# Expert weights in reading order, and one joined transfer for each contiguous stretch of the ring

## The chip, the cores and the metric

The kernel runs on one core of a Trainium2 chip. The metric is the time of one execution on the device in microseconds (us); it is measured in several runs and the median is given. A separate, profiled execution gives the trace.

## The reference, cut to what matters

One layer with 256 tokens of 512 numbers: cross-attention to a context of 4096 rows (16 heads), causal self-attention (16 heads), and a mixture of experts with 32 experts, of which each token chooses 4. The change concerns only how the weights of the experts come in. Each expert computes, for at most 10 rows gathered for it:

```python
G = jnp.einsum('ecd,edi->eci', Xp, W_gate)     # Xp (32, 10, 512), W_gate (32, 512, 256)
U = jnp.einsum('ecd,edi->eci', Xp, W_up)       # W_up (32, 512, 256)
Y = jnp.einsum('eci,eid->ecd', jax.nn.silu(G) * U, W_down)   # W_down (32, 256, 512)
Yf = Y.reshape(EC, d) * slots_w[:, None]
out = jnp.zeros((T, d), x.dtype).at[slots_token].add(Yf)
```

All of it is float32: 1.5 MB of weights an expert, 48 MB for 32 experts.

## The kernel before

The program is written out engine by engine. Five engines work through their own queues and wait for each other on semaphores. SyncE (SP) issues every load. A load adds 16 to its semaphore when all of it has landed.

**Layout of the weights.** The host lays out `w_exp` as (32 experts, 128 partitions, 3072 numbers): in each partition first the gate and up weights (`W_GU` = 2048 numbers, in four quarters of 512, one for each chunk `c` of 128 of the 512 input rows), then the down weights (2 × 512 numbers). So the gate/up part of one expert is 1 MB in 128 rows of 8 KB, a quarter of it is 256 KB in rows of 2 KB, and the down part is 512 KB in rows of 4 KB.

**Order of the experts.** The experts are read in groups of `GE` = 4, numbered by a reading index `k`; group `g` holds `k` = 4g to 4g+3. `expert(k)` (L116) says which expert is read as the `k`-th; it is a permutation, so neighbours in `k` are not neighbours in HBM.

**The ring.** SBUF has `RING` = 13 places for an expert's 3072 numbers a partition. Places 0 to 7 lie one after the other, 8 to 11 lie one after the other at another address, and 12 is by itself (L243). The expert with reading index `k` goes to place `k % 13`. Each place has a semaphore `ld_gu[k % 13]` for its gate/up part and `ld_down[k % 13]` for its down part (L319, L320).

**The loads** (SP, L400 to L449), one per expert and part:

- Places 0 to 7 after the cross-attention, 8 to 10 after its output product, 11 after the last transposes of the self-attention.
- Place 12 is shared with weights of the shared expert, so its load comes in pieces: the first half of gate/up once `sh_mm` is 1, the rest and the down part once `sh_mm` is 3.
- The other 19 experts (`k` = 13 to 31) refill freed places, in refill groups 0 to 4: `k` = 13-16, 17-20, 21-24, 25-28 and 29-31. Refill group `g` may be issued when TensorE has done group `g` (semaphore `gu_mm` for the gate/up part, `y_mm` for the down part). Group 0's gate/up parts are loaded a quarter at a time, as each chunk `c` of group 0 is done (`gu_part`). The order in the queue is: first half of `k` = 12, four quarters of group 0, gate/up of group 1, down of group 0, the rest of `k` = 12, down of group 1, gate/up and down of group 2, gate/up of groups 3 and 4, down of group 3, and last the down parts of group 4 in three parts (`END_PARTS`), three transfers each.

**Who reads them** (PE is TensorE). `gate_up(g, c)` (L1400) waits, for each of its four experts, for the gate/up semaphore of its place, in each of the four chunks `c`, and then multiplies at L1416. `down(g)` (L1432) waits for the down semaphores of its four experts and multiplies at L1444; for the last group it waits on `ld_end_down` part by part. Between the two, `hidden_back(g)` transposes the hidden values (L1429). The last stretch of TensorE's program is `gate_up(6)`, a part of the shared expert (L1369), `hidden_back(6)`, the adding of the rows (L1466, L1474), `gate_up(7)`, `down(6)`, `hidden_back(7)`, `down(7)`, and the combination (L1479). Group 6 is `k` = 24 to 27 and group 7 is `k` = 28 to 31.

Of the kernel before, what the change touches and what calls it, by code (L numbers as in the profile page):

```python
# [15 lines left out]
P = 128  # L16
# [3 lines left out]
DC = D // P  # L20
# [19 lines left out]
E = 32  # L40
# [4 lines left out]
GE = P // SLOT  # L45
NG = E // GE
W_GU = DC * 2 * FI
W_EXP = W_GU + FC * D
END_PARTS = [slice(W_GU, W_GU + D), slice(W_GU + D, W_GU + D + D // 2), slice(W_GU + D + D // 2, W_EXP)]
RING = 13  # L50
RING_LOW, RING_MID = 8, 11
# [1 line left out]
QK_BUFS, SM_BUFS, LAT_BUFS = 4, 5, 4  # L53
OUT_STEPS = H - LAT_BUFS
SH_FREES = 3
PIECED = GE
ENDING = RING + 4 * GE
XPW = E * CAP + SLOT - CAP
ROW_PARTS = [slice(0, 15), slice(15, E)]
# [56 lines left out]
def expert(k):  # L116

    trio, r = k // GE // 3, k // GE % 3
    each = min(3, NG - 3 * trio)
    return 12 * trio + each * (k % GE) + r  # L120


def gate_up_loaded(k):

    pieces = {RING - 1: 2, **{i: DC for i in range(RING, RING + PIECED)}}
    return 16 * sum(pieces.get(i, 1) for i in range(k % RING, k + 1, RING))


def wait(eng, sem, value):

    if isinstance(value, int) and value <= 0:
        return
    eng.wait_ge(sem, value)
# [12 lines left out]
def layer(nc, a, out):  # L146
    with ExitStack() as ctx:
        def sb(name, shape, dt=F32):
            return ctx.enter_context(nc.sbuf_tensor(name, shape, dt))
# [4 lines left out]
        def sem(name):  # L154
            return ctx.enter_context(nc.semaphore(name))
# [3 lines left out]
        arena = sb("arena", [P, 53200])  # L159

        def cut(cols, at=None):
            o = top[0] if at is None else at
            if at is None:
                top[0] += cols
            return arena[:, o:o + cols]
# [14 lines left out]
        q_at = top[0]  # L180
# [5 lines left out]
        r_at = top[0]  # L186
# [46 lines left out]
        high_at = r_at + (RING_MID - RING_LOW) * W_EXP  # L233
# [6 lines left out]
        rsum2 = arena[:, w_at + 1856:w_at + 1888].rearrange("p (s h) -> p s h", h=NH2)  # L240


        ring = [arena[:, o:o + W_EXP] for o in [W_EXP * e for e in range(RING_LOW)]  # L243
                + [r_at + W_EXP * e for e in range(RING_MID - RING_LOW)] + [high_at, q_at]]
        w_router = cut(DC * E).rearrange("p (c e) -> p c e", c=DC)
        bias_e = cut(E)
        sh_in = arena[:, q_at:q_at + 4096].rearrange("p (i n c k) -> p i n c k", i=DC, n=2, c=DC)
# [68 lines left out]
            sem(n) for n in ("q2_mm", "q2_done", "s2_mm", "s2_max", "s2_exp", "pT_mm", "pT_copied", "o2_mm", "o2_done",  # L316
                             "back_mm", "back_copied", "x2_mm"))
        ld_shared = [sem(f"ld_shared{i}") for i in range(2)]
        ld_gu = [sem(f"ld_gu{i}") for i in range(RING)]  # L319
        ld_down = [sem(f"ld_down{i}") for i in range(RING)]  # L320
        ld_end_down = [sem(f"ld_end_down{i}") for i in range(len(END_PARTS))]
        gu_part = sem("gu_part")
        cleared, logit_mm, sig_exp, sel_done, pos_mm, oh_done, ow_done, xp_mm, xp_copied = (
# [11 lines left out]
        def _(sp):  # L335
# [61 lines left out]
            sp.wait_ge(ctx_done, H)  # L397
            sp.dma_start(wo2, a["w_o2"]).then_inc(ld_wo2, 16)

            def load_expert(k, part, done):  # L400
                sp.dma_start(ring[k % RING][:, part], a["w_exp"][expert(k)][:, part]).then_inc(done[k % RING], 16)
            gate_up, down = slice(0, W_GU), slice(W_GU, W_EXP)

            def load_whole(k):
                load_expert(k, gate_up, ld_gu)
                load_expert(k, down, ld_down)
            for k in range(RING_LOW):
                load_whole(k)
            sp.wait_ge(o1_mm, OUT_STEPS + TT)
            for k in range(RING_LOW, RING_MID):  # L410
                load_whole(k)
            sp.wait_ge(q2_mm, NH2)
            sp.dma_start(sh_in, a["w_shared_in"].rearrange("p (i n c k) -> p i n c k", i=DC, n=2, c=DC)).then_inc(ld_shared[0], 16)
            sp.wait_ge(pT_mm, NH2)
            load_whole(RING_MID)
            sp.wait_ge(x2_mm, TT + 1)
            sp.dma_start(sd, a["w_shared_out"].rearrange("p (c n) -> p c n", c=DC)).then_inc(ld_shared[1], 16)
            def new(g):
                return range(RING + GE * g, min(RING + GE * (g + 1), E))

            def load_group(g, part, freed, done):
                sp.wait_ge(freed, g + 1)
                for k in new(g):
                    load_expert(k, part, done)
            quarters = [slice(2 * FI * c, 2 * FI * (c + 1)) for c in range(DC)]
            sp.wait_ge(sh_mm, 1)
            load_expert(RING - 1, slice(0, W_GU // 2), ld_gu)
            for c in range(DC - 1):
                sp.wait_ge(gu_part, c + 1)
                for k in new(0):  # L430
                    load_expert(k, quarters[c], ld_gu)
            load_group(0, quarters[DC - 1], gu_mm, ld_gu)
            load_group(1, gate_up, gu_mm, ld_gu)
            load_group(0, down, y_mm, ld_down)
            sp.wait_ge(sh_mm, SH_FREES)
            load_expert(RING - 1, slice(W_GU // 2, W_GU), ld_gu)
            load_expert(RING - 1, down, ld_down)
            load_group(1, down, y_mm, ld_down)
            last = (E - RING) // GE
            for g in range(2, last - 1):  # L440
                load_group(g, gate_up, gu_mm, ld_gu)
                load_group(g, down, y_mm, ld_down)
# [2 lines left out]
            load_group(last - 1, down, y_mm, ld_down)  # L445
            sp.wait_ge(y_mm, last + 1)
            for i, part in enumerate(END_PARTS):
                for k in new(last):
                    sp.dma_start(ring[k % RING][:, part], a["w_exp"][expert(k)][:, part]).then_inc(ld_end_down[i], 16)  # L449
            for n in range(2):  # L450
                half = slice(D // 2 * n, D // 2 * (n + 1))
                sp.wait_ge((x3_done, x3_second)[n], 1)
# [542 lines left out]
        def _(pe):  # L995
# [212 lines left out]
            for h in range(H + 2):  # L1208
# [3 lines left out]
                if 1 <= h <= H:  # L1212
                    g = h - 1
# [3 lines left out]
                if h >= 2:  # L1217
                    last = projected(h - 2, 0)
# [4 lines left out]
            for g in range(OUT_STEPS, H):  # L1223
                last = projected(g, TT - 1)
# [6 lines left out]
            for st in range(TT):  # L1231
# [109 lines left out]
            for st in range(TT):  # L1341
# [5 lines left out]
                for c in range(DC):  # L1347
                    last = mm(psA[0][:, E * st:E * st + E], xnT[:, c, P * st:P * st + P], w_router[:, c, :], start=c == 0, stop=c == DC - 1)
# [51 lines left out]
            def gate_up(g, c):  # L1400

                if g == 0:
                    pe.wait_ge(xp_copied, c + 1)
                    if c == 0:
                        pe.wait_ge(sh_done, 1)
                elif g == 3 and c == 0:
                    pe.wait_ge(xp_copied, 2 * DC)
                if c == 0:
                    wait(pe, hid_done, g - 1)
                for j in range(GE):  # L1410
                    k = GE * g + j
                    pe.wait_ge(ld_gu[k % RING], gate_up_loaded(k))
                for j in range(GE):
                    k = GE * g + j
                    e = expert(k)
                    last = mm(psF[g % 2][SLOT * j:SLOT * j + SLOT, :], xpT[:, c, CAP * e:CAP * e + SLOT], ring[k % RING][:, 2 * FI * c:2 * FI * (c + 1)],  # L1416
                              start=c == 0, stop=c == DC - 1)
                if c == DC - 1:
                    last.then_inc(gu_mm, 1)
                elif g < PIECED // GE:  # L1420
                    last.then_inc(gu_part, 1)

            def hidden_back(g):
# [8 lines left out]
            def down(g):  # L1432
                trio = g // 3
                pe.wait_ge(hT_copied, g + 1)
                wait(pe, y_copied, min(trio, TRIOS - 1))
                for j in range(GE):
                    k = GE * g + j
                    if k < ENDING:
                        pe.wait_ge(ld_down[k % RING], 16 * (k // RING + 1))
                def product(c, bank, out):  # L1440
                    for j in range(GE):
                        k = GE * g + j
                        o = W_GU + D * c
                        last = mm(bank[SLOT * j:SLOT * j + SLOT, out], hT[g % 3][:, c, SLOT * j:SLOT * j + SLOT], ring[k % RING][:, o + out.start:o + out.stop],  # L1444
                                  start=g % 3 == 0 and c == 0, stop=(g % 3 == 2 or g == NG - 1) and c == FC - 1, skip_group_check=True)
                    return last
                for c in range(FC):
                    if g == NG - 1 and c == 0:
                        pe.wait_ge(ld_end_down[0], 16 * (E - ENDING))
                    if trio < TRIOS - 1:  # L1450
                        last = product(c, psA[trio % 2], slice(0, D))
                    else:
                        for n in range(2):
                            if g == NG - 1 and c == FC - 1:
                                pe.wait_ge(ld_end_down[1 + n], 16 * (E - ENDING))
                            last = product(c, psA[n], halves[n])
                            if g == NG - 1 and c == FC - 1:
                                last.then_inc(y_mm, 1)
                if g < NG - 1:
                    last.then_inc(y_mm, 1)  # L1460
# [91 lines left out]
def lay_out(i):  # L1552
    g = {k: np.asarray(v) for k, v in i.items()}
    const, rope = constants()
    arrays = {"x": g["x"], "const": const, "rope": rope}
# [17 lines left out]
    pe = qb[:, :, NOPE:]  # L1573
# [9 lines left out]
    arrays["w_shared_out"] = shared[2].reshape(P, -1)  # L1583
    up = [g[f"L0_ffn_W_{n}"].reshape(E, DC, P, FI) for n in ("gate", "up")]
    down = g["L0_ffn_W_down"].reshape(E, FC, P, D).transpose(0, 2, 1, 3).reshape(E, P, -1)
    arrays["w_exp"] = np.concatenate([np.concatenate(up, 3).transpose(0, 2, 1, 3).reshape(E, P, -1), down], 2)
    return {k: np.ascontiguousarray(v) for k, v in arrays.items()}


# [11 lines left out]
```

## Time and profile before

| | us |
|---|---|
| median of 3 runs | 651.63 (649.9 to 651.67) |
| the profiled execution | 650.6 |
| its span (first to last instruction) | 648.7 |
| TensorE busy | 625.1 (96% of the span) |
| experts' multiplications, L1416 | 29.5 |

The profiled execution's own time is 1.9 us more than its span. A trace gives for every instruction its start and length, what ended the idle time before it, and for a load the time from its issue to its landing. A window's DMA share is the mean busy share of the 16 DMA engines, and GB/s is what they moved.

### The profile page before, as it was taken

Reading aid. Unit: us, or ns where it says so; the run is one execution under the profiler, and the core shown is the slowest. Engines: PE = TensorE matmul, PEld = TensorE weight load, DVE = VectorE, ACT = ScalarE, POOL = GpSimd, SP = SyncE. Lnnn points to the kernel's source line nnn. Section 1 sums busy time; section 2 is a strip of 40 time slices with the busy share of each in tenths; the row PEclk is TensorE's granted clock in tenths of the full one; section 3 lists DMA queues with packets and bytes.
Section 4 is the critical chain, followed back from the end, with each engine's and each line's share of the span. In section 5 each row is a group of like instructions: output and inputs, shape, how many; then the busy total and the mean of one; then the engine's idle time right before and its main releaser. Section 6 shows DMA issues by size and latency. Waiting matters only on the chain.

```text
span 648.7 us, 15224 instructions
## 1 busy us (share of the span) xinstructions
PE 625.1 (96%) x6035; PEld 466.0 (72%) x6035; DVE 378.8 (58%) x571; ACT 362.0 (56%) x494; POOL 177.7 (27%) x146
## 2 busy tenths in 40 slices
PE   7999999999999999999999999999999999999976
PEld 5986676777777778777777777899556897564443
DVE  5888587866767767767677676655214565501000
ACT  3543665777676677667667676788122874311000
POOL 0270334353453443443444434300000331000000
PEclk7999999999999999999999999999999999999999
DMA  8944884223423422422522521600999107499996
GB/s 338 419 171 94 219 317 98 58 56 74 82 51 65 90 49 59 99 49 51 107 49 43 116 50 36 125 2 3 379 417 371 80 2 250 151 398 411 420 417 224
DMA packets 28648, 105.14 MB, mean 162 GB/s; under 512 B 4288, under 2 KB 8896, under 8 KB 23488
## 3 DMA queue, kind: packets, MB, share of 16 engines
q1 hardware_dynamic: 28608, 104.57, 50.5%
q8 instruction: 30, 0.49, 0.3%
q14 instruction: 10, 0.08, 0.0%
HBM read 77.29 MB, written 0.52 MB: 120 GB/s over the span
## 4 chain that ended last, share of the span: by engine, by line
PE 82%; DVE 6%; issue 4%; ACT 3%; DMA 2%; SPq 2%; POOL 0%; DVEq 0%
PE psO L1128 9%; PE psO L1139 9%; PE psO L1129 8%; PE psS L1115 8%; PE psS L1116 8%; PE psM L1087 5%; PE psO L1207 4%; PE psS L1416 3%; PE psO L1071 3%; PE psS L1050 3%; PE psO L1042 2%; DVE arena L783 2%; SPq L449 2%; PE psO L1073 2%; PE psO L1072 2%
## 5 line engine op out<-in xcount | busy, mean ns | idle before, releaser
L783 DVE TENSOR_REDUCE arena<-psM 128x2 f32<-128x1024 f32 x121 | 147.7, 1221 | 67.4 <-PE psM L1087 67.1
L589 ACT ACTIVATE arena<-psS 128x1024 bf16<-128x1024 f32 x128 | 131.3, 1026 | 87.6 <-PE psS L1116 85.4
L482 POOL TENSOR_TENSOR arena<-arena 128x1024 bf16<-128x1024 f32 x56 | 120.8, 2156 | 190.4 <-ACT arena L591 166.9
L1128 PE MATMUL psO<-arena 128*128 128x129 bf16 x1024 | 132.8, 220 | 0.3 <-DVE arena L801 0.3
L1129 PE MATMUL psO<-arena 128*128 128x128 bf16 x1024 | 132.4, 220 | 0.0
L591 ACT ACTIVATE arena<-psS 128x1024 f32<-128x1024 f32 x129 | 131.0, 1017 | 0.0
L1115 PE MATMUL psS<-arena 128*128 128x256 bf16 x512 | 120.5, 273 | 0.9 <-DVE arena L794 0.9
L1116 PE MATMUL psS<-arena 65*128 65x256 bf16 x512 | 120.8, 273 | 0.0
L1128 PEld LDWEIGHTS psO<-arena 128*128 128x128 bf16 x1024 | 99.1, 98 | 18.8 <-issue 11.2
L1129 PEld LDWEIGHTS psO<-arena 128*128 128x128 bf16 x1024 | 99.4, 97 | 6.7
L822 DVE TENSOR_TENSOR arena<-arena 128x1024 bf16<-128x1024 f32 (+1 forms) x73 | 88.0, 1207 | 15.4 <-ACT arena L591 15.3
L1139 PE MATMUL psO<-arena 128*128 128x129 bf16 x1024 | 79.0, 220 | 0.2
L1139 PEld LDWEIGHTS psO<-arena 128*128 128x128 bf16 x1024 | 65.7, 97 | 2.8 <-DVE arena L822 1.1
L1115 PEld LDWEIGHTS psS<-arena 128*128 128x128 bf16 x512 | 50.2, 98 | 7.4 <-DVE arena L716 1.0
L1116 PEld LDWEIGHTS psS<-arena 65*128 65x128 bf16 x512 | 50.0, 98 | 5.4
L581 ACT CAST arena<-psO 128x512 bf16<-128x512 f32 x64 | 37.8, 591 | 24.5 <-PE psO L1073 24.3
L777 DVE TENSOR_TENSOR arena<-psO,arena 128x512 bf16<-128x512 f32 x64 | 43.8, 684 | 12.1 <-ACT arena L581 11.3
L1087 PE MATMUL psM<-arena 64*128 64x512 bf16 x242 | 47.2, 386 | 2.5 <-DVE arena L783 1.6
L1416 PE MATMUL psS<-arena 128*32 128x512 f32 x256 | 29.5, 595 | 4.2 <-DMA arena<-w_exp 4.2
L980 DVE TENSOR_TENSOR arena<-psS,arena 128x256 f32<-128x256 f32 x8 | 3.4, 424 | 47.1 <-ACT arena L670 47.1
L1207 PE MATMUL psO<-arena 128*128 128x512 f32 x64 | 30.2, 594 | 0.0
L1087 PEld LDWEIGHTS psM<-arena 64*128 64x128 bf16 x242 | 11.6, 93 | 22.5 <-issue 10.3
(209 smaller groups left out, 740.5 us busy)
## 6 DMA issues: line engine op xcount, KB each, us to landing
arena<-w_exp SPq DMA_DIRECT2D x27, 1024.0 KB, 19.6
arena<-arena SPq DMA_DIRECT2D x96, 256.0 KB, 3.7
arena<-w_exp SPq DMA_DIRECT2D x31, 512.0 KB, 16.8
arena<-w_pair SPq DMA_DIRECT2D x7, 1088.0 KB, 18.3
arena<-w_exp SPq DMA_DIRECT2D x19, 256.0 KB, 6.0
arena<-w_o SPq DMA_DIRECT2D x1, 4096.0 KB, 18.2
arena<-ctx SPq DMA_DIRECT2D x4, 512.0 KB, 13.1
arena<-rope SPq DMA_DIRECT2D x4, 512.0 KB, 13.9
```

Of the source, the lines that this page charges most:

```text
L482: nc.gpsimd.tensor_tensor(p_lo[:, s % 2, :], p_f[:, s % 2, :], p_hi[:, s % 2, :], ALU.subtract).then_inc(s_plo[0], 1)
L589: nc.scalar.activation(p_hi[:, s % 2, :], psS[s % 2][:, :], ACT.Exp).then_inc(s_phi, 1)
L591: nc.scalar.activation(p_f[:, s % 2, part], psS[s % 2][:, part], ACT.Exp).then_inc(s_pf, 1)
L783: nc.vector.reduce_max(maxes[:, :, st, c], maxima_bank(q, m)[:, :].rearrange("p (j n) -> p j n", j=2), AX.X).then_inc(s_mfree, 1)
L822: nc.vector.tensor_tensor(p_lo[:, s % 2, part], p_f[:, s % 2, part], p_hi[:, s % 2, part], ALU.subtract).then_inc(s_plo[s % 2], 1)
L1087: last = mm(bank[:, 512 * j:512 * j + 512], queries_of[r, P * st:P * st + P], k_hi[r, 512 * c:512 * c + 512], start=True, stop=True)
L1115: mm(o, k1[:, j, l], q1[:, j, :], start=True, stop=False)
L1116: last = mm(o, k2[0:R + 1, j, l], q2[0:R + 1, j, :], start=False, stop=True)
L1128: mm(psC[:, st, :], ph, vx[:, GROUP * g + i, 0:CW], start=g == 0 and i == 0 and st == 0, stop=False, skip_group_check=True)
L1129: last = mm(psC[:, st, 0:K], ph, vx[:, GROUP * g + i, CW:VW], start=False, stop=False, skip_group_check=True)
L1139: last = mm(psC[:, st, :], p_lo[:, s % 2, T * i + P * st:T * i + P * st + P], vx[:, GROUP * g + i, 0:CW], start=False, stop=g == HALF - 1 ...
L1207: return mm(psO[st][:, :], latT[:, g % LAT_BUFS, P * st:P * st + P], wo1[:, g, :], start=g == 0, stop=g == H - 1)
```

## The change

The host stores the experts in reading order, so that `k` is the index in HBM. The ring's stretches that are contiguous in SBUF and filled together become runs, `(first, end)`: (0,4), (4,8), (8,11), (11,12), (12,13) at the start, and then (13,17), (17,21), (21,25), (25,26) and (26,29), (29,32), one refill group each except the fourth, which goes over the ring's end. One transfer loads the same part of all experts of a run. A run has one semaphore for gate/up and one for down, and its readers wait for the run's transfer at the first expert of each group and at the first expert of each run. `SP`'s waits for freed places and the order of the transfers in the queue stay.

```diff
-def gate_up_loaded(k):
+def refills(g):
+
+    ks = range(RING + GE * g, min(RING + GE * (g + 1), E))
+    turn = [k for k in ks if k % RING == 0 and k > ks[0]]
+    return [(ks[0], turn[0]), (turn[0], ks[-1] + 1)] if turn else [(ks[0], ks[-1] + 1)]
+
+REFILLS = [refills(g) for g in range((E - RING + GE - 1) // GE)]
+RUNS = [(0, GE), (GE, RING_LOW), (RING_LOW, RING_MID), (RING_MID, RING - 1), (RING - 1, RING)] + [run for group in REFILLS for run in group]
+
+def run_of(k):
+
+    return next(first for first, end in RUNS if first <= k < end)
+
+def gate_up_loaded(first):
 
-    pieces = {RING - 1: 2, **{i: DC for i in range(RING, RING + PIECED)}}
-    return 16 * sum(pieces.get(i, 1) for i in range(k % RING, k + 1, RING))
+    pieces = {RING - 1: 2, RING: DC}
+    return 16 * sum(pieces.get(f, 1) for f, _ in RUNS if f <= first and f % RING == first % RING)
+
+def down_loaded(first):
+
+    return 16 * sum(1 for f, _ in RUNS if f <= first and f % RING == first % RING)
...
-            def load_expert(k, part, done):
-                sp.dma_start(ring[k % RING][:, part], a["w_exp"][expert(k)][:, part]).then_inc(done[k % RING], 16)
+            def load_run(run, part, done):
+                first, end = run
+                o = ring_at[first % RING]
+                places = arena[:, o:o + W_EXP * (end - first)].rearrange("p (k w) -> p k w", w=W_EXP)
+                sp.dma_start(places[:, :, part], a["w_exp"][first:end, :, part].rearrange("k p w -> p k w")).then_inc(done, 16)
...
-            for k in range(RING_LOW):
-                load_whole(k)
+            for run in RUNS[0:2]:
+                load_whole(run)
...
                 sp.wait_ge(freed, g + 1)
-                for k in new(g):
-                    load_expert(k, part, done)
+                for run in REFILLS[g]:
+                    load_run(run, part, done[run[0] % RING])
...
             for i, part in enumerate(END_PARTS):
-                for k in new(last):
-                    sp.dma_start(ring[k % RING][:, part], a["w_exp"][expert(k)][:, part]).then_inc(ld_end_down[i], 16)
+                load_run(REFILLS[last][0], part, ld_end_down[i])
...
-                    pe.wait_ge(ld_gu[k % RING], gate_up_loaded(k))
+                    if j == 0 or run_of(k) == k:
+                        pe.wait_ge(ld_gu[run_of(k) % RING], gate_up_loaded(run_of(k)))
...
-                    if k < ENDING:
-                        pe.wait_ge(ld_down[k % RING], 16 * (k // RING + 1))
+                    if k < ENDING and (j == 0 or run_of(k) == k):
+                        pe.wait_ge(ld_down[run_of(k) % RING], down_loaded(run_of(k)))
...
-                        pe.wait_ge(ld_end_down[0], 16 * (E - ENDING))
+                        pe.wait_ge(ld_end_down[0], 16)
...
-    arrays["w_exp"] = np.concatenate([np.concatenate(up, 3).transpose(0, 2, 1, 3).reshape(E, P, -1), down], 2)
+    arrays["w_exp"] = np.concatenate([np.concatenate(up, 3).transpose(0, 2, 1, 3).reshape(E, P, -1), down], 2)[[expert(k) for k in range(E)]]
```

## Rows read from the trace of the kernel before

**Rows 1.** The page: its span, part 1's TensorE row, part 2's DMA slices.
```profile
span 648.7 us, 15224 instructions
...
PE 625.1 (96%) x6035; PEld 466.0 (72%) x6035; DVE 378.8 (58%) x571; ACT 362.0 (56%) x494; POOL 177.7 (27%) x146
...
DMA  8944884223423422422522521600999107499996
```

**Rows 2.** Waits of TensorE, 556 to 649 us: total us, times, longest.
```profile
PE psS L1416 <- DMA arena<-w_exp: 4.2, 2, 3.5
...
PE psM L1444 <- DMA arena<-w_exp: 1.5, 3, 1.0
```

**Rows 3.** Chain that ended last, 618 to 649 us: start, us, what.
```profile
633.63 9.21 DMA arena<-w_exp
642.85 0.04 issue
642.89 0.64 PE psM L1444 x8
```

**Rows 4.** Windows: engines' busy us, clock, DMA share, GB/s.
```profile
510.00:520.00 10.00, 10.00 (x71) 9.12 (x70) 6.57 (x26) 7.67 (x17) 2.88 (x4) 1.00 0.00 0
...
563.00:565.00 2.00, 2.00 (x18) 0.87 (x20) 0.00 (x0) 0.39 (x2) 0.00 (x0) 1.00 0.65 199
565.00:571.00 6.00, 6.00 (x58) 1.76 (x54) 0.42 (x1) 1.07 (x4) 0.00 (x0) 1.00 0.99 324
571.00:575.00 4.00, 4.00 (x30) 2.58 (x23) 0.42 (x1) 0.33 (x2) 0.00 (x0) 1.00 1.05 397
...
588.00:598.00 10.00, 8.71 (x67) 4.83 (x69) 1.54 (x3) 1.51 (x4) 0.00 (x0) 1.00 1.03 410
600.00:609.00 9.00, 9.00 (x67) 4.46 (x66) 0.33 (x1) 0.61 (x2) 0.00 (x0) 1.00 1.01 418
...
641.00:642.00 1.00, 1.00 (x20) 0.54 (x24) 0.00 (x0) 0.00 (x0) 0.00 (x0) 1.00 0.12 41
```

**Rows 5.** DMA of 557 to 643 us: packets and bytes, the instruction queue.
```profile
DMA packets 8501, 31.54 MB, mean 367 GB/s; under 512 B 944, under 2 KB 1712, under 8 KB 6576
...
q8 instruction: 5, 0.08, 0.4%
```

**Rows 6.** Timeline of SP, five single issues: start, us, then the issue.
```profile
1.19 0.42 SPq L346 DMA_DIRECT2D arena<-x  x1
...
600.69 0.43 SPq L401 DMA_DIRECT2D arena<-w_exp  x1
...
601.17 6.30 SPq L401 DMA_DIRECT2D arena<-w_exp  x1
...
610.00 1.05 SPq L401 DMA_DIRECT2D arena<-w_exp  x1
...
615.74 0.44 SPq L401 DMA_DIRECT2D arena<-w_exp  x1
```

**Rows 7.** The last four's issue to landing, in their order: KB, us.
```profile
arena<-w_exp SPq DMA_DIRECT2D x1, 1024.0 KB, 23.1
...
arena<-w_exp SPq DMA_DIRECT2D x1, 1024.0 KB, 25.1
...
arena<-w_exp SPq DMA_DIRECT2D x1, 1024.0 KB, 23.7
...
arena<-w_exp SPq DMA_DIRECT2D x1, 512.0 KB, 23.1
```

**Rows 8.** Timeline of TensorE, 618 to 649 us: start, us, line, count, [idle before].
```profile
618.46 1.93 PE L1444 MATMUL psM<-arena 128*32 128x512 f32 x16 [0.32 <-ACT arena L678]
...
623.89 3.64 PE L1416 MATMUL psS<-arena 128*32 128x512 f32 x32 [3.51 <-DMA arena<-w_exp]
...
633.84 3.64 PE L1416 MATMUL psS<-arena 128*32 128x512 f32 x32 [0.71 <-DMA arena<-w_exp]
...
637.67 1.93 PE L1444 MATMUL psM<-arena 128*32 128x256 f32 x32 [0.20 <-DMA arena<-w_exp]
639.53 0.44 PE L1429 MATMUL psS<-arena 128*128 128x128 f32 x2
...
640.96 1.57 PE L1444 MATMUL psM<-arena 128*32 128x256 f32 x24 [0.99 <-DMA arena<-w_exp]
...
643.46 2.00 PE L1479 MATMUL psO<-arena 128*128 128x256 f32 x8
```

More of the change, by code:

```diff
@@ L55 @@
 SH_FREES = 3
-PIECED = GE
 ENDING = RING + 4 * GE
@@ L240, in layer @@
         rsum2 = arena[:, w_at + 1856:w_at + 1888].rearrange("p (s h) -> p s h", h=NH2)
-        ring = [arena[:, o:o + W_EXP] for o in [W_EXP * e for e in range(RING_LOW)]
-                + [r_at + W_EXP * e for e in range(RING_MID - RING_LOW)] + [high_at, q_at]]
+        ring_at = [W_EXP * e for e in range(RING_LOW)] + [r_at + W_EXP * e for e in range(RING_MID - RING_LOW)] + [high_at, q_at]
+        ring = [arena[:, o:o + W_EXP] for o in ring_at]
         w_router = cut(DC * E).rearrange("p (c e) -> p c e", c=DC)
@@ L318, in layer @@
         ld_shared = [sem(f"ld_shared{i}") for i in range(2)]
-        ld_gu = [sem(f"ld_gu{i}") for i in range(RING)]
-        ld_down = [sem(f"ld_down{i}") for i in range(RING)]
+        starts = sorted({first % RING for first, _ in RUNS})
+        ld_gu = {i: sem(f"ld_gu{i}") for i in starts}
+        ld_down = {i: sem(f"ld_down{i}") for i in starts}
         ld_end_down = [sem(f"ld_end_down{i}") for i in range(len(END_PARTS))]
@@ L398, in _, with load_whole @@
             sp.dma_start(wo2, a["w_o2"]).then_inc(ld_wo2, 16)
-            def load_expert(k, part, done):
-                sp.dma_start(ring[k % RING][:, part], a["w_exp"][expert(k)][:, part]).then_inc(done[k % RING], 16)
-            gate_up, down = slice(0, W_GU), slice(W_GU, W_EXP)
-            def load_whole(k):
-                load_expert(k, gate_up, ld_gu)
-                load_expert(k, down, ld_down)
-            for k in range(RING_LOW):
-                load_whole(k)
+            def load_run(run, part, done):
[3 more added lines that the diff above has]
+                sp.dma_start(places[:, :, part], a["w_exp"][first:end, :, part].rearrange("k p w -> p k w")).then_inc(done, 16)
+            gate_up, down = slice(0, W_GU), slice(W_GU, W_EXP)
+            def load_whole(run):
+                load_run(run, gate_up, ld_gu[run[0]])
+                load_run(run, down, ld_down[run[0]])
+            for run in RUNS[0:2]:
+                load_whole(run)
             sp.wait_ge(o1_mm, OUT_STEPS + TT)
-            for k in range(RING_LOW, RING_MID):
-                load_whole(k)
+            load_whole(RUNS[2])
             sp.wait_ge(q2_mm, NH2)
@@ L414, in _ @@
             sp.wait_ge(pT_mm, NH2)
-            load_whole(RING_MID)
+            load_whole(RUNS[3])
             sp.wait_ge(x2_mm, TT + 1)
             sp.dma_start(sd, a["w_shared_out"].rearrange("p (c n) -> p c n", c=DC)).then_inc(ld_shared[1], 16)
-            def new(g):
-                return range(RING + GE * g, min(RING + GE * (g + 1), E))
             def load_group(g, part, freed, done):
                 sp.wait_ge(freed, g + 1)
-                for k in new(g):
-                    load_expert(k, part, done)
+                for run in REFILLS[g]:
+                    load_run(run, part, done[run[0] % RING])
+            held = (RING - 1, RING)
             quarters = [slice(2 * FI * c, 2 * FI * (c + 1)) for c in range(DC)]
             sp.wait_ge(sh_mm, 1)
-            load_expert(RING - 1, slice(0, W_GU // 2), ld_gu)
+            load_run(held, slice(0, W_GU // 2), ld_gu[RING - 1])
             for c in range(DC - 1):
                 sp.wait_ge(gu_part, c + 1)
-                for k in new(0):
-                    load_expert(k, quarters[c], ld_gu)
+                load_run(REFILLS[0][0], quarters[c], ld_gu[0])
             load_group(0, quarters[DC - 1], gu_mm, ld_gu)
@@ L435, in _ @@
             sp.wait_ge(sh_mm, SH_FREES)
-            load_expert(RING - 1, slice(W_GU // 2, W_GU), ld_gu)
-            load_expert(RING - 1, down, ld_down)
+            load_run(held, slice(W_GU // 2, W_GU), ld_gu[RING - 1])
+            load_run(held, down, ld_down[RING - 1])
             load_group(1, down, y_mm, ld_down)
-            last = (E - RING) // GE
+            last = len(REFILLS) - 1
             for g in range(2, last - 1):
@@ L1419, in gate_up @@
                     last.then_inc(gu_mm, 1)
-                elif g < PIECED // GE:
+                elif g == 0:
                     last.then_inc(gu_part, 1)
@@ L1454, in down @@
                             if g == NG - 1 and c == FC - 1:
-                                pe.wait_ge(ld_end_down[1 + n], 16 * (E - ENDING))
+                                pe.wait_ge(ld_end_down[1 + n], 16)
                             last = product(c, psA[n], halves[n])
```

## The prediction

> **What bounds the kernel now.** I read the page first: TensorE is busy in 96% of the span of 648.7 us, but the DMA digits are 9 in the slices before the last [rows 1]. So there may be a stage in which TensorE is nearly full and the loads set the end. The waits of the last 93 us name it: TensorE stands 4.2 us at L1416 and 1.5 us at L1444 for `w_exp` and hardly anywhere else [rows 2]. The chain that ended last goes from the last weights transfer, issued at 633.63 and landed at 642.85, straight into the last eight multiplications [rows 3]. The windows say how full the stream of weights is: from 565 us on, the DMA share is 1.0, at 324, then 397, 410 and 418 GB/s [rows 4]. Between 557 and 643 us, 31.5 MB go through, 20 experts' weights [rows 5]. Even at 418 GB/s these take 75 us, so the end is the start of this stream, plus bytes over rate, plus some 6 us of work behind the last landing. TensorE is late only in its last two groups: group 6 starts at 623.89 after 3.51 us of waiting, group 7 at 633.84 after 0.71 us [rows 8]. The first 11 experts are no matter: from 510 to 520 us the DMA share is 0.00, everything issued until then has landed [rows 4], and no wait on them is among [rows 2].
>
> **The change part by part.** The rows of 8, 4 and 2 KB stay what they are, in each expert's own 12 KB rows; what is joined is four transfers of 128 rows into one of 512. The sum is made on the profiled execution (650.6 us).
>
> *Fewer transfers.* 557 to 643 us has 944 small packets, 16 a transfer, so 59 transfers [rows 5]. After: first half of `k` = 12 (1), four quarters (4), groups 1 (2), 0's down (1), rest of `k` = 12 (2), group 2 (2), group 3 in two runs (4), group 4's gate/up (1), the last three parts (3): 20. So 39 go. What does a transfer cost beside its bytes? A 1 MB one at 418 GB/s (600 to 609 us) takes 2.51 us, 512 KB at 410 (588 to 598) takes 1.28, 256 KB at 397 (571 to 575) takes 0.66 [rows 4]. Halving leaves 2 × 1.28 − 2.51 = 0.05 us, and 2 × 0.66 − 1.28 = 0.04 us. This fixed part belongs to the transfer or to its 128 rows, for each engine has 8 rows and one small packet of each. If all is the transfer's, 39 × 0.05 = 1.9 us are gained; if all is the rows', nothing. I take it as spread evenly over the nine packets: 39 × 0.05 / 9 = 0.2 us gained.
>
> The Trainium skill weighs in here ("DMA: Bandwidth & Descriptors", the section on the anatomy of one DMA, and its rules for kernel authors): some 2.0 us fixed for each DMA, and many small transfers are to be coalesced. Taken as a cost of each transfer in the stream it would give 78 us for the 39, more than the whole stream; these rows show transfers queued behind each other, with 0.05 us between them, so here that cost is latency, which the queue hides.
>
> *The start of the stream.* The four quarters of group 0 are now four issues and not sixteen. They move 324 GB/s from 565 to 571 us where later 2 KB rows move 397 [rows 4]: 6 × (397 − 324) = 0.44 MB, or 1.1 us late; from 563 to 565 us, 2 × (397 − 199) = 0.40 MB, 1.0 us late. If SP's issues were the cause, up to 2.1 us would come back, and everything behind would land that much earlier. But the share in 565 to 571 is 0.99 [rows 4]: the engines were not idle, their packets took longer, which a quicker issue doesn't mend. I take 0.3 us. On the other side, one transfer of 512 rows could be slower to begin: if its issue of 0.43 us grew with the rows, the first would come 1.3 us later. The load of `x`, 256 rows in one issue, took 0.42 us, no longer than one of 128 rows (0.43) [rows 6], so I put this at nothing and keep 1.3 us as the loss end.
>
> *The coarser waits.* Now a group also waits for experts of the next group that share its run: group 4 for `k` = 20, group 5 for 24, group 6 for 28. For groups 4 and 5 all has long landed, as TensorE does not wait there [rows 2]. In group 6 it counts. Before, `k` = 27 landed at 600.69 + 23.1 = 623.8 and L1416 began at 623.89. `k` = 28 landed at 601.17 + 25.1 = 626.3 [rows 6, 7], 2.5 us later, so group 6 begins at 626.4. What follows without a wait takes 633.84 − 0.71 − 623.89 = 9.24 us [rows 8], so group 7 begins at 635.6, not 633.84 (its own weights landed at 610.00 + 23.7 = 633.7 [rows 6, 7]): 1.8 us late. Then 3.6 us at L1416: `down(6)` can start at 639.2. It now needs `k` = 28's down part too, landed at 615.74 + 23.1 = 638.8 [rows 6, 7]: no wait. It takes 1.86 us (637.67 to 639.53), the transposes 0.38, their way over ScalarE back to L1444 0.32 [rows 8]: `down(7)` starts at 641.8 and not 640.96, and its first 24 multiplications, 1.57 us before, end at 643.4, its last eight at some 643.7 against 643.53. The copy of the first half of its result takes 0.4 us on VectorE, so the combination starts at about 643.8 against 643.46 [rows 8]. Lost: 0.3 us. So 2.5 us of new wait are nearly swallowed by the waits for the last parts (0.99 and 0.36 us) and the 0.91 us that group 7 and `down(6)` stood. Bounds: 0 and, if nothing swallowed it, 2.5. If the stream gets earlier by d, both limits move by d, and so does the end.
>
> *Waits and instructions on TensorE.* 157 waits become 74. They lie beside multiplications in progress (L1416 has no idle but for DMA [rows 2]), so they cost nothing before or after. 83 instructions fewer move the moments at which instructions are fetched: five packets of 16 KB in these 86 us [rows 5], each 16384 B / (418 GB/s / 16) = 0.6 us of one engine. The last landing is one engine's: at 641 to 642 us the share is 0.12, two engines of 16 [rows 4]. So whether such a packet meets the latest engine moves the end by 0.6 us either way; I take nothing.
>
> *HBM layout.* An engine now goes from a row to the same row of the next expert, 1.5 MB on, before the next partition 12 KB on. No row of this trace has such a stride, so its nearest bounds are the rates of this stream itself: 418 GB/s, unchanged, and 397, the lowest that a full share shows late in it [rows 4]. All engines step to the next expert together, so the distances between engines stay; I take no change. Joined are 18 of 20 experts, 28.3 MB: 68.2 us at 415, 71.3 at 397, so 3.1 us is the loss end.
>
> The skill's page "DMA: Bandwidth & Descriptors", section "Latency and other measured facts", speaks against the change: copies with a row pitch of 512 KiB ran at 207 GB/s and of 2 MiB at 164, with a padded pitch at 214. Taken over to this stride, an estimate from that page is 3 to 30% more time for the joined loads, 2 to 20 us. No row here can show it; it was measured for the pitch between partitions, which here stays 12 KB.
>
> Sum: 650.6 − 0.2 − 0.3 + 0.3 = 650.4. The profiled execution was 1.03 us below the median of the runs, so as a median 651.63 − 0.2 = 651.4 us.
>
> **The rivals.**
>
> *The stream starts earlier.* SP's sixteen short issues did hold the early quarters back: −2.1 − 0.2 + 0.3 = −2.0, 649.6 us. For it: 199 and 324 GB/s just where the issues are dense; against it: the share of 0.99.
>
> *The fixed part is the transfer's.* −1.9 − 0.3 + 0.3 = −1.9, 649.7 us. For it: it is the same 0.04 to 0.05 us at three sizes; against it: the rows a transfer are the same at all three.
>
> *Slower: rows 1.5 MB apart come at a lower rate.* Price up to 3.1 us, with the 0.3 us of waiting and the 0.2 gained 3.2: 654.8 us. It decides from a loss of 2.7% of the rate on, which is 1.9 us; it would show in all windows from 577 us on.
>
> *Not joined.* The three-dimensional transfer is split again into one per expert. The gain of 0.2 and of the start is lost, the wait stays: +0.3, 651.9 us. Against it: `x` is loaded in two rows a partition in one issue [rows 6].
>
> **How the numbers follow.** Forecast 0.59, earlier start 0.12, fixed part 0.10, slower rate 0.13, not joined 0.06. A measurement of this kernel tells a change from none at about 0.3%, 2.0 us (below 649.7, above 653.6). The first two rivals lie on that edge and pass it if they come together with each other or with a lucky instruction fetch: 0.20 for faster, with a little from the forecast's own spread. Slower is the fourth case, 0.13. The forecast's own range is 650.0 to 652.8 (the terms' 0.3 us, the fetch's 0.6 us, the coarser wait, the median's own spread). The range for 8 in 10 goes down to the two faster rivals and a bit below, 648.9, and up into the rate loss, 653.8.
>
> **What would show it.** Right: 20 issues of `w_exp` from 557 us on; 416 to 422 GB/s where 8 KB rows run; L1416 of group 6 starts about 2.5 us after its old distance to the stream, with an idle of some 6 us; L1444's waits for DMA near zero; the last landing within 1 us of 642.9. The 0.3 us of the start is wrong if 565 to 571 us shows some 397 GB/s. The prediction fails if the rate from 577 us on differs by over 2%, if TensorE waits in group 4 or 5, or if a joined transfer leaves engines idle while SP stands in its issue.

## The result, and the profile after

| | before | after |
|---|---|---|
| median, 22 runs each, beside each other | 649.51 us (648.17 to 651.67) | 651.63 us (649.3 to 653.34) |
| ratio of the runs | | 1.0021, 95% interval 1.0011 to 1.0031 |
| profiled execution; its span | 650.6; 648.7 | 650.83; 649.0 |

The change makes the kernel slower: by the ratio of the runs 0.2% or 1.4 us (0.7 to 2.0 by its interval); the medians lie 2.1 us apart, the means 1.6 (649.65 and 651.20 us). The ratio lies within the 0.3% that the forecast took for "no change", but its interval excludes 1, and the forecast had it 0.2 us faster. The median that the forecast started from (3 runs) was itself 2 us above that of 22 runs; what counts is the difference.

The two spans differ by 0.3 us only, because the two executions began differently. In the first 18 us the granted clock was lower for longer in the profile of before: the mean from 7 to 18 us is 0.53 before, 0.69 after (windows; the granted clock, as a share of 2.4 GHz, is the third number from the end). Before:

```profile
7.00:18.00 11.00, 8.86 (x34) 7.83 (x34) 6.70 (x16) 4.05 (x7) 2.02 (x1) 0.53 1.02 417
```

After:

```profile
7.00:18.00 11.00, 9.29 (x48) 7.96 (x48) 7.42 (x17) 5.94 (x10) 1.84 (x1) 0.69 1.03 412
```

This hides 1.1 us. So all profiles are compared below from one common point, the issue of the first quarter of refill group 0: 562.51 us before, 561.43 after. From there to the end of the span it is 86.2 us before and 87.6 after, 1.4 us more. Two more profiles of each kernel, below, give 86.6 and 86.0 before, 87.0 and 87.1 after, so that the means of three lie 1.0 us apart.

SP's timeline (start, us) of the kernel after: the first quarter, the fourth, the gate/up run (26, 29), and the last part.

```profile
561.43 0.39 SPq L425 DMA_DIRECT2D arena<-w_exp  x1
...
565.70 0.38 SPq L425 DMA_DIRECT2D arena<-w_exp  x1
...
598.40 0.44 SPq L425 DMA_DIRECT2D arena<-w_exp  x1
...
627.02 4.31 SPq L425 DMA_DIRECT2D arena<-w_exp  x1
```

And the way to landing of the last three of these (KB, us):

```profile
arena<-w_exp SPq DMA_DIRECT2D x1, 1024.0 KB, 9.7
...
arena<-w_exp SPq DMA_DIRECT2D x1, 3072.0 KB, 26.1
...
arena<-w_exp SPq DMA_DIRECT2D x1, 384.0 KB, 14.1
```

The last part lands at 627.02 + 14.1 = 641.1, 79.7 us after the first issue; before it was 642.85 − 562.51 = 80.3 [rows 3]. The loads got earlier, by 0.7 us. What got longer is the way from the last landing to the end: 5.9 us before, 7.9 after. TensorE's timeline says why (start, us, idle before in brackets; L1436 was L1416, L1464 was L1444, L1388 was L1369, L1499 was L1479; the rows answer to [rows 8]):

```profile
624.61 5.45 PE L1436 MATMUL psS<-arena 128*32 128x512 f32 x32 [5.30 <-DMA arena<-w_exp]
629.99 2.00 PE L1388 MATMUL psO<-arena 128*128 128x256 f32 x8
...
635.59 3.64 PE L1436 MATMUL psS<-arena 128*32 128x512 f32 x32
639.05 1.91 PE L1464 MATMUL psM<-arena 128*32 128x256 f32 x32
...
641.64 1.93 PE L1464 MATMUL psM<-arena 128*32 128x256 f32 x32 [0.32 <-ACT arena L697]
643.76 2.00 PE L1499 MATMUL psO<-arena 128*128 128x256 f32 x8 [0.18 <-DVE arena L996]
```

Group 6 waits 5.30 us and not 3.51, as its wait is now for `k` = 28 too (598.40 + 26.1 = 624.5). Then its 32 multiplications take 5.45 us, not 3.64. The windows show the granted clock (third number from the end), in the idle time and in the work behind it:

```profile
620.00:621.00 1.00, 0.00 (x0) 0.00 (x0) 0.07 (x1) 0.00 (x0) 0.00 (x0) 1.00 0.98 410
621.00:622.00 1.00, 0.00 (x0) 0.00 (x0) 0.00 (x0) 0.00 (x0) 0.00 (x0) 0.74 1.01 418
622.00:623.00 1.00, 0.00 (x0) 0.00 (x0) 0.00 (x0) 0.00 (x0) 0.00 (x0) 0.50 1.04 434
...
625.00:626.00 1.00, 1.00 (x8) 0.23 (x4) 0.00 (x0) 0.00 (x0) 0.00 (x0) 0.50 0.98 410
...
629.00:630.00 1.00, 1.00 (x13) 0.15 (x5) 0.00 (x0) 0.00 (x0) 0.00 (x0) 1.00 0.97 397
```

TensorE goes idle at 619.3; from 621.5 on its clock is granted at half, 1.2 and not 2.4 GHz; it resumes at 624.6 and has the full clock back only at 628.3. In the kernel before, the clock was at 1.00 from 616 to 630 us, its 3.5 us of idle time included. The multiplications of group 7, of `down(6)` and `down(7)` then have no wait on `w_exp` left: the waits of 0.71, 0.20, 0.99 and 0.36 us that stood there before are used up.

### The profile page after: what moved, and what is told of

Its sections match the earlier page's. It is cut to its first block, busy times and chain, and to the rows that moved or that the text cites. A ratio compares the mean times of both kernels' runs of the same rounds, so it can differ in the third digit from the quotient of the medians.

```text
span 649.0 us, 15126 instructions
## 1 busy us (share of the span) xinstructions
PE 626.6 (97%) x6035; PEld 466.0 (72%) x6035; DVE 379.5 (58%) x571; ACT 361.9 (56%) x494; POOL 178.6 (28%) x146
## 4 chain that ended last, share of the span: by engine, by line
PE 82%; DVE 6%; DMA 5%; issue 4%; ACT 3%; SPq 0%; POOL 0%; DVEq 0%
PE psO L1147 9%; PE psO L1158 9%; PE psO L1148 8%; PE psS L1134 8%; PE psS L1135 8%; PE psM L1106 5%; DMA arena<-w_exp 4%; PE psO L1226 4%; PE psS L1436 4%; PE psO L1090 3%; PE psS L1069 3%; DVE arena L802 2%; PE psO L1061 2%; PE psO L1092 2%; PE psO L1091 2%
## 5 line engine op out<-in xcount | busy, mean ns | idle before, releaser
L1436 PE MATMUL psS<-arena 128*32 128x512 f32 x256 | 31.3, 626 | 5.3 <-DMA arena<-w_exp 5.3
```

## The experiments

Theory A: the coarser wait of group 6 costs the time, for the most part through the TensorE clock, which falls in the longer idle time. Rival B: the joined transfers themselves cost it. Rival C: group 6's later start costs it by itself, whatever the clock. Each experiment was timed beside the kernel before, and its ratio is to that. "From the first quarter" means: span, less the issue of the first quarter.

### The coarser wait alone

```diff
                     pe.wait_ge(ld_gu[k % RING], gate_up_loaded(k))
+                if g == 6:
+                    pe.wait_ge(ld_gu[28 % RING], gate_up_loaded(28))
```

> The kernel before, all transfers as before, with one wait more: group 6's gate/up multiplications (L1416) also wait for the gate/up part of k = 28. Theory A (the loss is the coarser wait, and most of it the TensorE clock, which falls in the longer idle time and makes group 6's multiplications take 5.4 us and not 3.6): idle before group 6 some 5.9 us, granted clock 0.50 in part of it, L1416 x32 at 5.4 us, time 1.5 to 2.1 us over the kernel before. Rival B (the joined transfers themselves cost the time, the wait is swallowed as forecast): 0 to 0.3 us over the kernel before.

Measured: ratio 1.0029 (1.0015 to 1.0043), medians 651.52 against 649.81. From the first quarter 87.4 us, within 0.2 us of the changed kernel. Its timeline (L1418 was L1416) and its clock from 616 to 630 us:

```profile
625.99 5.21 PE L1418 MATMUL psS<-arena 128*32 128x512 f32 x32 [5.42 <-DMA arena<-w_exp]
```
```profile
616.00:630.00 14.00, 8.26 (x54) 3.31 (x54) 1.11 (x2) 0.61 (x2) 0.00 (x0) 0.88 1.01 420
```

One wait more, with all 59 transfers as before, makes the whole loss. Rival B falls. The clock fell later here than in the first profile of the changed kernel: at 625.8 us, 0.2 before TensorE resumed.

### The run cut at `k` = 28

```diff
+REFILLS[3] = [(25, 26), (26, 28), (28, 29)]
```

> The changed kernel with the run (26, 29) cut into (26, 28) and (28, 29), so that group 6 waits for its own experts alone. Theory A: idle before group 6 some 3.0 us (3.5 before, less what the stream gained at its start), granted clock 1.00 in 616 to 630, L1436 x32 at 3.6 us; time 1.5 to 2.1 us below the changed kernel, 0.3 to 0.7 below the kernel before. Rival B: time stays at the changed kernel's, 1.4 us over the kernel before.

Measured: ratio 0.9991 (0.9979 to 1.0003), median 648.76. From the first quarter 85.2 us, 2.4 less than the changed kernel. The wait is shorter, as expected, but the clock fell here too, against the expectation (L1437 was L1416, L1465 was L1444):

```profile
621.67 5.13 PE L1437 MATMUL psS<-arena 128*32 128x512 f32 x32 [2.46 <-DMA arena<-w_exp]
...
632.34 3.64 PE L1437 MATMUL psS<-arena 128*32 128x512 f32 x32
...
638.79 1.53 PE L1465 MATMUL psM<-arena 128*32 128x256 f32 x24 [0.72 <-DMA arena<-w_exp]
640.67 0.64 PE L1465 MATMUL psM<-arena 128*32 128x256 f32 x8 [0.36 <-DMA arena<-w_exp]
```

It cost nothing that the profile shows: the last parts are still waited for behind it (0.72, 0.36 us), and the end comes 5.84 us after the last landing, as before (5.87). So the fall is dear only where the slack in front of the last landing has been spent.

### The wait filled

```diff
             for g in range(2, NG):
+                if g == 6:
+                    warm(22, psF[1])
```

`warm(n, psF[1])` issues n bf16 multiplications that need no load and whose results are overwritten later.

> The changed kernel with 22 bf16 multiplications of 128 x 128 by 128 x 512 (results overwritten later) ahead of group 6's wait, some 4.7 us of work in the 5.3 us of idle time; no wait is shortened. Theory A with the clock as its cause: granted clock 1.00 throughout, L1436 x32 at 3.6 us, time 1.8 us below the changed kernel, some 0.4 below the kernel before. Rival C (the later start of group 6 costs the 1.4 us by itself, whatever the clock): time within 0.4 us of the changed kernel.

Measured: ratio 1.0000 (0.9987 to 1.0012), median 650.03. The filling is L1020:

```profile
620.61 4.92 PE L1020 MATMUL psS<-arena 128*128 128x512 bf16 x22
626.18 3.64 PE L1436 MATMUL psS<-arena 128*32 128x512 f32 x32 [0.66 <-DMA arena<-w_exp]
```
```profile
616.00:630.00 14.00, 13.03 (x85) 5.58 (x82) 1.12 (x2) 0.73 (x3) 0.00 (x0) 1.00 1.01 421
```

Group 6 starts as late as in the changed kernel (63.4 us after the first quarter, there 63.2), the clock is full, and the kernel is as fast as the one before. Rival C falls: the late start is nearly harmless, the clock is what hurts. The end comes 6.15 us after the last landing, against 5.87 before and 7.89 in the changed kernel.

### Only the four quarters joined

```diff
-                for k in new(0):
-                    load_expert(k, quarters[c], ld_gu)
+                load_quarter(c)        # one transfer for k = 13 to 16, weights in reading order
```

> The kernel before with the experts stored in reading order and only the four quarters of refill group 0 joined (16 transfers are 4); all other transfers and all waits as before. If the start of the stream gains because SP no longer spends sixteen issues on it: landing of the last quarter 14.0 us after the first issue instead of 14.5, last landing 0.5 us earlier counted from that issue, time 0.3 to 0.6 us below the kernel before. If the gain needs all transfers joined: landings as before, time within 0.2 us of the kernel before.

Measured: ratio 1.0000 (0.9987 to 1.0014), median 649.51. The last quarter landed 14.7 us after the first issue, not earlier than before (14.5), so four issues in place of sixteen did not speed up the quarters here. Yet the last landing was at 79.2 us, as early as in kernels with all transfers joined. One profile doesn't settle a term this small; what all of them say together is below.

### Cut and filled; the kernel before, filled

The cut kernel with `warm(10, psF[1])` ahead of group 6, and the kernel before with `warm(14, psF[1])` there.

> The changed kernel with the run (26, 29) cut at 28, and 10 bf16 multiplications (2.2 us, results overwritten later) ahead of group 6's wait. If the clock's fall in that idle time is the only loss left, which the cut alone still showed in its profile (3.4 us at 0.50 after 2.5 us of idle time): clock 1.00, L1436 x32 of group 6 at 3.6 us, time 0 to 1.0 us below the cut alone (648.8), 1.0 to 1.8 us below the kernel before. If the fall there is harmless because the last transfers swallow it: time as with the cut alone, within 0.3 us.

> The kernel before with 14 bf16 multiplications (3.1 us) in its own 3.5 us of idle time ahead of group 6. Its runs lie between 648.3 and 652.0 us with different mean clocks. If part of that spread is a clock that falls in this idle time: median 0.3 to 0.7 us below the kernel before and fewer runs at a mean clock of 0.989 or less. If its spread comes from the start of the program alone: same median within 0.2 us.

Measured: 0.9992 (0.9975 to 1.0009), median 649.81, and 1.0002 (0.9988 to 1.0017), median 650.44, beside 650.22 of the kernel before. Both profiles have L1416's 32 at 3.64 us and a clock of 1.00. Neither gains anything that intervals of about 1 us to each side would show; the gain of 1.0 us or more that was expected of the first did not come. Where the last parts are waited for, a clock held up is worth little.

### Filled in part, at the beginning of the wait

`warm(8, psF[1])` in the changed kernel.

> The changed kernel with 8 bf16 multiplications (1.8 us) at the beginning of group 6's idle time, which leaves 3.5 us of it idle, as long as before. If the loss grows with the idle time that TensorE has before group 6: clock falls in some runs only, median between the changed kernel (651.6) and the one with the wait filled (650.0), some 650.5 us. If any work in the wait is enough: 650.0. If filling must be complete: 651.6.

Measured: ratio 1.0023 (1.0006 to 1.0039), median 651.43: as the changed kernel.

```profile
620.37 1.90 PE L1020 MATMUL psS<-arena 128*128 128x512 bf16 x8
625.16 5.34 PE L1436 MATMUL psS<-arena 128*32 128x512 f32 x32 [2.89 <-DMA arena<-w_exp]
```

2.89 us of idle time behind the filling went with a fall, less than the 3.51 us that the first profile of the kernel before went through at full clock. The clock fell at 625.8 us, 0.6 after TensorE had resumed. It is not a matter of the idle time's length alone.

### The changed kernel once more, and the kernel before twice more

> The changed kernel, unaltered, profiled once more. Theory A: end of group 6's multiplications late by the clock (L1436 x32 at 4.5 to 5.5 us), or, in a run of mean clock 0.992 or more, at 3.6 us with a span some 1.8 us shorter than the first profile's. Rival B: L1436 at 3.6 us and the span no shorter.

> The kernel before, unaltered, profiled once more. If its 3.5 us of idle time never bring the clock down: L1416 of group 6 at 3.6 us, clock 1.00 from 18 us to its end. If they do in part of the runs, this one may show 5.2 us, with a span over 1 us longer counted from the first quarter's issue.

> As the run above, a third profile of the kernel before; the same two readings.

Measured, from the first quarter to the end: 87.0 us for the changed kernel. Its clock fell at 624.4 us, 0.2 after TensorE had resumed, and the 32 multiplications took as much longer:

```profile
624.22 5.34 PE L1436 MATMUL psS<-arena 128*32 128x512 f32 x32 [4.88 <-DMA arena<-w_exp]
```
```profile
624.00:625.00 1.00, 0.78 (x8) 0.29 (x12) 0.00 (x0) 0.00 (x0) 0.00 (x0) 0.69 1.04 434
625.00:626.00 1.00, 1.00 (x12) 0.42 (x8) 0.00 (x0) 0.00 (x0) 0.00 (x0) 0.50 0.94 393
```

For the kernel before 86.6 and 86.0. The second profile of it shows the clock falling in its own 3.4 us of idle time:

```profile
624.22 6.33 PE L1416 MATMUL psS<-arena 128*32 128x512 f32 x32 [3.42 <-DMA arena<-w_exp]
...
636.08 3.64 PE L1416 MATMUL psS<-arena 128*32 128x512 f32 x32
```
```profile
616.00:630.00 14.00, 10.27 (x62) 3.71 (x58) 1.12 (x2) 0.61 (x2) 0.00 (x0) 0.76 1.01 421
```

The third does not (L1416 at 3.64 us). So the kernel before meets the same fall in part of its executions. It makes L1416 2.7 us longer, and the end 0.3 and 0.6 us later than in the two profiles without it, since 2.3 us of waits for weights stood behind it.

### The filling put behind the wait for group 6's own weights

```diff
+                if g == 6 and c == 0:
+                    warm(10, psF[1])
+                    pe.wait_ge(ld_gu[28 % RING], gate_up_loaded(28))
```

> The kernel before with the coarser wait of group 6 for k = 28, and 10 bf16 multiplications (2.2 us) between the arrival of group 6's own weights and that wait: 3.5 us idle as in the kernel before, then busy until k = 28 has landed. If idle time beyond that of the kernel before is what brings the clock down: L1416 x32 of group 6 at 3.6 us in most runs, time within 0.3 us of the kernel before. If 3.5 us of idle time and a later start are enough: L1416 at 5.2 us, time 1 to 1.5 us over the kernel before.

Measured: ratio 1.0012 (0.9994 to 1.0030), median 651.49: inconclusive by the time. The profile shows the fall at 622.6 us, in the idle time, and the filling itself (L1001) at the low clock:

```profile
623.45 4.42 PE L1001 MATMUL psS<-arena 128*128 128x512 bf16 x10 [2.93 <-DMA arena<-w_exp]
627.81 4.40 PE L1419 MATMUL psS<-arena 128*32 128x512 f32 x32
```

Ten multiplications take 4.42 us, where ten took 2.33 at full clock in the cut kernel, and `k` = 28 had landed at 625.8: filling that comes after the fall makes group 6 later still, 88.5 us from the first quarter, the longest of all.

### What joining is worth, with the wait filled in both

The kernel before with the coarser wait and `warm(22, psF[1])`, one transfer per expert. It differs from the changed kernel with its wait filled in two things at once, the joined transfers and the order of the experts in HBM.

> The kernel before, its transfers one per expert, with the coarser wait of group 6 for k = 28 and 22 bf16 multiplications (4.9 us) ahead of it: the same wait and the same filling as the changed kernel with its wait filled (1.0000 of the kernel before), so that the two differ in the joined transfers and the order in HBM alone. If joining is worth nothing: clock 1.00, ratio to the kernel before 0.999 to 1.001. If joining gives what the forecast had in it (0.5 us): 0.3 to 0.7 us over the kernel before, that is about 1.0008. If it gives the 2 us of the faster rivals: over 1.0025.

Measured: 1.0015 (0.9996 to 1.0034), median 650.39 beside 650.15; which by itself tells little. Four kernels were then timed on one chip, beside each other: the changed one, the changed one filled, this one, and the cut one.

> The changed kernel, timed beside the three below. If the clock's fall before group 6 costs it 1.1 to 1.6 us as the profiles say: 0.7 to 1.6 us over f2, with more runs of a mean clock of 0.989 or less.

> The changed kernel with 22 bf16 multiplications in group 6's wait, timed beside f3, which has the same wait and filling with one transfer per expert. If joining and the order in HBM are worth nothing: within 0.3 us of f3. If joining is worth the forecast's 0.5 us or more: that much below f3.

> One transfer per expert, coarser wait of group 6, 22 bf16 multiplications in it. Worth of joining nothing: as f2. Worth 0.5 us: 0.5 us over f2. Worth 2 us, as the two faster rivals had it: 2 us over f2.

> The changed kernel with its run (26, 29) cut at 28. If the coarser wait is the whole loss: 1.0 to 2.0 us below f1 and, with the wait of the kernel before, 0 to 0.8 us below the kernel before. If the loss were in the joined transfers: as f1.

| on one chip | median | ratio to before (649.82) |
|---|---|---|
| changed (7 runs) | 652.31 | 1.0046 (1.0029 to 1.0062) |
| changed, wait filled (12) | 649.88 | 1.0002 (0.9988 to 1.0016) |
| one transfer per expert, same wait, filled (12) | 650.75 | 1.0014 (1.0000 to 1.0028) |
| changed, cut at 28 (12) | 650.01 | 1.0007 (0.9989 to 1.0026) |

The profile of the changed kernel taken here is its third: 87.1 us from the first quarter, L1436's 32 at 5.34 us behind 4.98 us of idle time. Filling the wait takes 2.4 us off the changed kernel, more than the 0.7 to 1.6 that were expected, the cut 2.3; the intervals of the changed kernel and of the filled one lie apart. Joining and the order in HBM together are worth 0.9 us by the medians, with intervals that overlap. The mean clock of the runs is a rough count of the falls, since it also holds the low clock at the program's start, whose length varies: at 0.989 or less were 40 of 117 runs of the kernel before, 20 of 29 of the changed one, 7 of 12 with the coarser wait alone, but 1 of 47 in the four timings with 22 fillers in the same wait; of the cut kernel, 9 of 23. It misses some: the second and the third profile of the changed kernel show a fall at a mean clock of 0.992 and 0.995. Among the 22 runs of the changed kernel, the 6 at 0.992 have a mean of 649.7 us, the 11 at 0.989 one of 651.5, the 5 at 0.987 one of 652.4; part of these steps is the start's.

## Why the prediction was wrong

*The step that failed* is in "the coarser waits": "What follows without a wait takes 633.84 − 0.71 − 623.89 = 9.24 us". These 9.24 us, from the start of group 6 to that of group 7, begin with group 6's 32 multiplications at L1416, 3.64 us in a row behind 3.51 us of idle time at a granted clock of 1.00. The forecast put them behind 6 us of idle time as if the clock came along. In all five profiles with the coarser wait and nothing or 1.9 us of filling ahead of it (the changed kernel three times, the wait alone, the wait filled in part) the 32 took 5.2 to 5.5 us, and the stretch 10.7 to 11.0. In the four with the wait filled they took 3.64, and the stretch 9.2. The "3.6 us at L1416" of group 7 held in all of them. The missing term is 1.6 us at the end: it comes 7.7 to 7.9 us after the last landing in the five, and 5.9 to 6.2 in the four.

The wait itself was right in kind and forecast too long. Group 6 was to begin 2.5 us later; counted from the first quarter's issue it began 1.8 us later in the changed kernel (63.2 us, before 61.4) and 1.9 with the wait alone. The idle time was 4.9 to 5.4 us and not "some 6". The bound of 0 to 2.5 us for the whole term does hold the 1.9 us that it cost; but its upper end stood for a wait that nothing swallowed, not for a slower TensorE, and no rival did.

The Trainium skill has this as a rule in "TensorE: Matmul & The Clock Gate", sections "HAM oscillation" and "Why this matters for your kernels": an idle gap between bursts of multiplications, such as a wait for a load, can put TensorE back to half its clock. With this rule, a fall of the clock in the lengthened wait would have been a rival with a price. The traces agree on the direction: of the 18 profiles, none of the 6 with at most 1.03 us of idle time ahead of group 6 shows a fall, 5 of the 8 with 2.3 to 3.5 us do, and all 4 with 4.9 to 5.4 us. But a fall was seen behind 2.5 us and none behind 3.5 us, so the length alone does not decide.

*The coarser wait at full clock.* Forecast 0.3 us lost. From last landing to end: 5.84 to 5.87 us in the profiles where group 6 waits for its own weights and the clock holds, 6.12, 6.15 and 6.23 in three of four with the coarser wait filled, 5.85 in the fourth. Right, 0.3 us, and with it the reason: the waits behind swallow the rest. That they were thereby spent, so that the next delay would count in full, was in the numbers and not drawn from them. The kernel before paid about 0.5 us for a fall of the clock, the changed one pays 1.6.

*Fewer transfers and the start of the stream.* Forecast 0.2 and 0.3 us gained. Over 17 profiles, leaving out the one with only the quarters joined, the last landing is 80.1 us after the first quarter's issue in the 8 with one transfer per expert (79.8 to 80.7) and 79.4 in the 9 with joined ones (79.0 to 79.8): 0.7 us gained, against the 0.5 of both terms. Of it, 0.4 lie before the last quarter has landed (14.4 and 14.0 us) and 0.3 behind. The two rivals that gave 2 us fall. This gain is the difference between two groups of profiles and rests on no single one; the timing on one chip (0.9 us) points the same way. From 565 to 571 us the changed kernel moved 368 GB/s, where 324 were moved before [rows 4] and 397 would have spoken against the term of 0.3 us:

```profile
565.00:571.00 6.00, 6.00 (x58) 1.66 (x50) 0.85 (x2) 0.99 (x3) 0.00 (x0) 1.00 1.02 368
```

That joining is what gains is not shown. All nine joined kernels also store the experts in reading order, and the profile left out, which has this order and 47 transfers, had its last landing at 79.2 us too, though its last quarter landed at 14.7. So the order in HBM is a rival for this gain that no run sets apart. The 2.0 us for each DMA, which the prediction takes from the Trainium skill ("DMA: Bandwidth & Descriptors", the section on the anatomy of one DMA), are stated there for transfers that GpSimd issues, and here SyncE issues all.

*HBM layout.* No loss. The window of 4 KB rows from 588 to 598 us moves 415 GB/s (410 before [rows 4]), that of 8 KB rows from 600 to 609 us 412 (418 before; 416 to 422 were expected, and 2% was the limit), that from 616 to 630 us 420.

```profile
588.00:598.00 10.00, 8.70 (x68) 4.12 (x67) 1.12 (x2) 1.41 (x3) 0.00 (x0) 1.00 1.04 415
600.00:609.00 9.00, 9.00 (x67) 4.43 (x66) 0.42 (x1) 0.61 (x2) 0.00 (x0) 1.00 1.00 412
...
616.00:630.00 14.00, 8.38 (x55) 2.51 (x54) 0.69 (x1) 0.23 (x1) 0.00 (x0) 0.76 1.01 420
```

The estimate of 2 to 20 us from the row pitches in the Trainium skill ("DMA: Bandwidth & Descriptors", section "Latency and other measured facts") did not come about: transfers that step 1.5 MB from expert to expert and 12 KB from partition to partition move 412 to 420 GB/s, as the stream did before (410 to 419).

*Joined at all?* Yes: 20 issues, 320 small packets, 16 for each, and 7557 others, as many as before [rows 5].

```profile
DMA packets 7877, 31.54 MB, mean 367 GB/s; under 512 B 320, under 2 KB 1088, under 8 KB 5952
```

*Sum.* −0.7 + 0.3 + 1.6 = 1.2 us. The first two profiles lie 1.4 us apart from the first quarter on, the means of three 1.0, and the ratio of the runs says 1.4 (0.7 to 2.0). The medians are wider apart: 2.1 us in the first timing and 2.5 in the one on one chip, where filling the wait took 2.4 us off. No profile shows what the rest would be. The slower rival was the wrong one; the place, group 6, was named, with a price of 0.3 us.

What stays open is what decides in one execution whether the clock falls, with the same idle time at the same place; and whether any version beats the kernel before. The cut at 28 keeps the earlier stream and has the old wait, but its two timings, 0.9991 (0.9979 to 1.0003) and 1.0007 (0.9989 to 1.0026), cannot be told from 1.

## What to carry to other kernels

When transfers are joined, ask for each reader whether it now waits for something that it doesn't read; cut the joined run at the reader's own boundary where loads are what it waits for. A longer wait of TensorE costs its length and, behind it, perhaps a clock at half: price the work behind a long wait at both levels. And slack is one account: what swallows the first delay is not there for the second, so add up delays before comparing them with it.

## What the runs showed of the hardware

An issue can stand for long while earlier transfers are still under way. That of one of the joined last parts stood 15.0 us, where the longest before was 6.3; the DMA share was 1.01 meanwhile (616 to 630 us).

```profile
611.97 15.00 SPq L425 DMA_DIRECT2D arena<-w_exp  x1
```

The issues of the four joined quarters, 512 rows each, took 0.38 to 0.39 us, no longer than one of 128 rows that did not stand (0.34 to 0.43).
